# A post-norm decoder layer on one core: the queries' low part, the projection bias and the row scatters change their places

## What is computed

```python
x = _layernorm(x + _L0_attn_ref(x, ...))                 # a decaying linear attention, then a feed-forward
x = _layernorm(x + _L0_xattn_ref(x, ctx, ctx, mask, ...)) # 16 heads of 8 columns, softmax over the context
x = _layernorm(x + _L0_ffn_ref(x, Wr, W1, b1, W2, b2))    # 8 experts, the best 2 of each row
```

## Time and profile before

| | us |
|---|---|
| median of 3 runs | 801.77 |
| lowest, highest | 800.95, 807.67 |
| the profiled execution | 798.83 |
| its span | 797.0 |
| one loop pass (289.81 to 354.77) | 64.96 |
| TensorE busy, VectorE, ScalarE, GpSimd | 670.7, 512.8, 400.8, 320.8 |

### The profile page before, as it was taken

How to read it: one execution, slowest core, us unless ns; L and a number is a source line. 1 busy time by engine, 2 the same in 40 slices (tenths; PEclk the granted TensorE clock), 3 DMA queues, 4 the chain that set the end, 5 groups by cost and what they waited for, 6 DMA issues and landing times.

```text
span 797.0 us, 19859 instructions
## 1 busy us (share of the span) xinstructions
PE 670.7 (84%) x6190; PEld 502.2 (63%) x6190; DVE 512.8 (64%) x1733; ACT 400.8 (50%) x855; POOL 320.8 (40%) x463
## 2 busy tenths in 40 slices
PE   9789979888997987988888899798576999999920
PEld 9565636745854763764674585476353799999920
DVE  4687477767667768667676766766546355555535
ACT  0312555464474374465547347446240477777726
POOL 6104560363264165057136326405404255544535
PEclk8579997999998999899899899899575999999965
DMA  8500000000000000000000000000022222222144
GB/s 295 195 15 1 22 21 3 2 24 17 0 20 20 0 20 20 0 1 33 7 0 20 20 0 20 20 0 7 22 107 68 70 69 73 71 66 74 57 157 181
DMA packets 26058, 36.23 MB, mean 45 GB/s; under 512 B 7302, under 2 KB 18311, under 8 KB 25736
## 3 DMA queue, kind: packets, MB, share of 16 engines
q1 hardware_dynamic: 20582, 22.72, 9.2%
q0 software_dynamic: 4576, 9.53, 3.4%
q10 hardware_dynamic: 850, 3.38, 1.3%
HBM read 23.99 MB, written 12.63 MB: 46 GB/s over the span
## 4 chain that ended last, share of the span: by engine, by line
PE 53%; DVE 20%; issue 12%; POOL 5%; ACT 4%; DMA 2%; SPq 1%; another core or an unknown queue 1%; DVEq 1%; ACTq 0%; POOLq 0%
PE bank L1543 8%; PE bank L1858 8%; PE bank L1868 8%; PE bank L1708 4%; POOL rstd L737 3%; PE bank L1579 3%; PE bank L1677 3%; PE bank L1695 3%; DVE stats L1044 2%; ACT mix L555 2%; PE bank L1627 2%; PE bank L1716 2%; DVE negmax L1169 2%; PE bank L1635 2%; PE bank L1730 1%
## 5 line engine op out<-in xcount | busy, mean ns | idle before, releaser
L734 POOL TENSOR_SCALAR vare<-mv 128x1 f32<-128x1 f32 (+1 forms) x108 | 23.9, 221 | 267.2 <-DVE mv L1049 266.9
L856 POOL DMA_INDIRECT expert_out<-xa,v_sb x71 | 68.3, 962 | 77.2 <-issue 47.2
L675 ACT ACTIVATE hT<-bank,qT 128x128 f32<-128x128 f32 x284 | 81.0, 368 | 36.3 <-issue 19.8
L1169 DVE TENSOR_REDUCE negmax<-bank 128x4 f32<-128x512 f32 x128 | 80.2, 684 | 21.8 <-PE bank L1677 12.6
L555 ACT ACTIVATE mix<-bank 128x512 f32<-128x512 f32 x128 | 66.1, 603 | 36.9 <-PE bank L1695 36.6
L779 POOL DMA_INDIRECT expert_in<-xb_rows,slot_u x72 | 71.9, 999 | 31.1 <-issue 18.5
L1868 PE MATMUL bank<-w_t,hT 128*128 x568 | 75.5, 276 | 1.1 <-DVE xa L1389 0.5
L1858 PE MATMUL bank<-xnT,qT 128*128 128x128 f32 x568 | 75.1, 275 | 0.4 <-issue 0.4
L1868 PEld LDWEIGHTS bank<-w_t,hT 128*128 128x128 f32 x568 | 69.1, 192 | 2.0 <-issue 1.8
L737 POOL TENSOR_TENSOR rstd<-vare,minus_half 128x1 f32<-128x1 f32 (+1 forms) x108 | 66.5, 615 | 9.6 <-POOL vare L734 1.2
L1858 PEld LDWEIGHTS bank<-xnT,qT 128*128 128x128 f32 x568 | 69.0, 192 | 0.6 <-issue 0.6
(11 more groups left out here) (300 smaller groups left out, 1490.9 us busy)
## 6 DMA issues: line engine op xcount, KB each, us to landing
v_sb<-expert_in SPq DMA_DIRECT2D x71, 66.0 KB
w_t<-in_w_t ACTq DMA_DIRECT2D x1, 2064.0 KB, 7.5
x_all<-in_x SPq DMA_DIRECT2D x4, 512.0 KB, 7.7
xT_all<-in_xT SPq DMA_DIRECT2D x4, 512.0 KB, 8.3
ctxT<-in_ctxT SPq DMA_DIRECT2D x8, 256.0 KB, 2.9
w_t<-in_w_t SPq DMA_DIRECT2D x1, 2048.0 KB, 7.5
x_all<-expert_out SPq DMA_DIRECT2D x4, 512.0 KB, 10.0
mix<-expert_out SPq DMA_DIRECT2D x3, 512.0 KB, 7.4
```

The lines of the kernel that those rows point to most:

```text
L675: ins = nc.scalar.activation(hx[j % 2][:, c, :], bank[2 + j % 2][:, c * P:(c + 1) * P], ACT.Gelu, bias=w1c[j % 2][:, FF + c:FF + c + 1])
L856: nc.gpsimd.indirect_dma_start(ys[:, :], bass.IndirectOffsetOnAxis(ap=tag[j % ROWS][:, HOME - P:HOME - P + 1].bitcast(U32), axis=0), ysb[j ...
L1169: nc.vector.tensor_reduce(negmax[t % 2][:, i, 28:28 + XC], b[:, :].rearrange("p (c n) -> p c n", c=XC), AX.X, ALU.max, negate=True).then_i ...
```

## The change

On VectorE, `first_sums` can call a function when its four second sums are out and ahead of the statistics of tile 3 and the moments of tiles 2 and 3; in the seven loop passes `queries_low(g)` is called there, in the last group it stays where it was. On GpSimd, the eight scatters are issued one at a time with other work or a wait between them; three of the gaps hold a wait for a job of TensorE (`mx2i0`, `mT2`, `mT3`) and an increment of a semaphore that nobody reads; `xab` moves from behind the LNA scales to behind the fifth scatter and `ff_residual`.

```diff
-            def row_out(t):
-                for k in range(TOPK):
+            def row_out(t, ways=range(TOPK)):
+                for k in ways:
                     nc.gpsimd.indirect_dma_start(
                         xs[:, :], bass.IndirectOffsetOnAxis(ap=slot_u[:, t, k:k + 1], axis=0),
                         xb_rows[k][:, t, :], None).then_inc(scattered, 16)
...
             def group(g, last=False):
                 if not last:
                     first_sum_in(g + 2)
-                row_out(0)
+                row_out(0, [0])
                 if not last:
                     heb_residual(g + 1)
+                row_out(0, [1])
+                if not last:
                     gammas(g + 1)
                 ln_scale(LNA, g, 0)
                 ln_scale(LNA, g, 1)
                 ln_scale(LNA, g, 2)
                 ln_scale(LNA, g, 3)
+                row_out(1, [0])
+                if not last:
+                    ln_scale(LN2, g + 2, 0, T)
+                row_out(1, [1])
+                if not last:
+                    filled(pool, g, f"ks{XC - 1}")
+                    masks(g + 1)
+                row_out(2, [0])
+                if not last:
+                    ff_residual(g + 1)
                 pool.wait_ge(xn_ready[LNA], ln_nth(g, T - 1) + 1)
                 nc.gpsimd.tensor_tensor(
                     xab[:, :, :], xa[:, :, :],
                     bo_bc[:, :].unsqueeze(1).broadcast_to([P, T, P]), ALU.add).then_inc(xab_ready, 1)
                 if not last:
-                    ln_scale(LN2, g + 2, 0, T)
-                row_out(1)
-                row_out(2)
-                if not last:
-                    filled(pool, g, f"ks{XC - 1}")
-                    masks(g + 1)
-                row_out(3)
-                if not last:
-                    ff_residual(g + 1)
+                    filled(pool, g, "mx2i0")
+                pool.sem_inc(pool_held, 1)
+                row_out(2, [1])
+                if not last:
+                    filled(pool, g, "mT2")
+                pool.sem_inc(pool_held, 1)
+                row_out(3, [0])
+                if not last:
+                    filled(pool, g, "mT3")
+                pool.sem_inc(pool_held, 1)
+                row_out(3, [1])
+                if not last:
                     ln_scale(LN3, g + 1, 0)
...
-            def first_sums(k):
+            def first_sums(k, between=None):
...
                 for t in range(T + 2):
+                    if t == T and between:
+                        between()
                     if t < T:
...
                 def next_sums():
                     dve.wait_ge(x1b_ready, g + 2)
-                    first_sums(g + 2)
+                    first_sums(g + 2, lambda: queries_low(g))
...
                 if not last:
                     next_sums()
-                queries_low(g)
+                else:
+                    queries_low(g)
                 placed_queries(g, 1)
                 placed_queries(g, 3)
```

## The result

| | before | after |
|---|---|---|
| median | 803.13 (4 runs) | 768.02 (4 runs, 764.54 to 772.6) |
| the profiled execution, its span | 798.83, 797.0 | 772.6, 770.7 |
| loop passes (VectorE's loop branch to its next) | 64.5 to 65.6 | 60.2 to 60.4 |

All ratios here are the recorded ones, from executions in the fast state, and can differ a little from the quotient of the medians. The seven passes are 4.7 us shorter each, 33 us in all. The two profiled executions differ by 26 us only, because the last group and the expert phase took 5.6 us longer in that of the kernel after.

What follows compares the result with a forecast made beforehand. TensorE, busy 670.7 of 797.0 us, bounds the kernel, so gains come from its idle time. Seven passes at 1.34 us give 9.4: 789.4 from the profiled execution, 792.4 from the median, forecast 791, range 775 to 801.

Steps and rivals of the forecast that it cites:

- Part 1: VectorE's first sums (L1060): with `xab` gone from beside them, a hold of 1.03 us a pass ends.
- Part 2: VectorE: `low` ahead of three statistics and moments instructions can start 0.54 us earlier a pass; those three cost nothing.
- Together: `low` must wait for ScalarE's `high`, so it starts 1.34 us earlier; seven passes give 9.4 us, the last group 0.
- Part 3: GpSimd: scatters issued one at a time, later `xab` and three waits for TensorE change nothing: 0.
- the direct parts: Freeing the first sums from `xab` and moving `low` ahead of the moments: 9.4 us over seven passes.
- Rival (a): VectorE's stall before the second maxima, some 13.1 us, goes too once scatters are spread: 778 us; chance 0.12.
- (b): TensorE's low clock behind that stall shortens or goes: 9 us more gives 782, 18 more 773; chance 0.12.
- The low clock stays: The forecast kept the half-speed clock behind the second-maxima stall, costing about 2.6 us a pass; forecast's chance 0.55.
- Rival (d): The low clock lasts twice as long in each pass, over the attention work: 9 us slower, 809; chance 0.07.

Runs made afterwards that it cites:

- e2: Only `xab` moved, behind the packed scatters and `ff_residual`, against the kernel before on chip 3: 759.57 us, ratio 0.9893.
- e1: Only `queries_low` moved ahead of the last moments, GpSimd in its old order, against the kernel before on chip 3: 762.47 us, ratio 0.9928.
- e6: The whole change, unchanged, against the kernel before on chip 5: 758.74 us, ratio 0.9871.
- e11: Only the scatters issued one at a time with the three waits, `xab` and `low` unmoved, against the kernel before on chip 1: 777.09 us, ratio 0.9657.
- e12: The whole change without its three waits and increments, last three scatters in a row, against the kernel before on chip 1: 767.58 us, ratio 0.9545.
- e5: The kernel before, unchanged, run as a kernel of its own on chip 5: 769.38 us, ratio 0.9998.
- e8: Only the six packed scatters moved, behind the third turned maxima with one added wait, against the kernel before on chip 9: 846.27 us, ratio 1.0584.
- e10: The kernel before, unchanged, profiled on chip 9: 797.18 us in one execution.
- e7: `low` ahead of the moments and `xab` moved, scatters still packed, against the kernel before on chip 9: 794.98 us, ratio 0.9957.
- e15: The whole change without its three waits and increments, against the kernel before on chip 14: 768.47 us, ratio 0.9624.
- e13: The change with its scatters as four pairs instead of eight single ones, against the kernel before on chip 1: 801.49 us, ratio 0.9968.
- e14: The whole change once more, against the kernel before on chip 14: 765.91 us, ratio 0.9593.

## Why the prediction was wrong, point by point

- **Part 1, L1060 freed by `xab`: right.** The four take 1.13 us beside a scatter where 1.1 had been worked out; e2 alone brought 8.2 us where 7.2 were priced. The prediction also read the rule of the Trainium skill (SBUF — State Buffer, the practical consequences) strictly, so that a scatter's issue would block the sum as `xab` did. That reading did not hold: 1.13 us beside the scatter at 347.61.
- **Part 2, `low` ahead of the moments: right.** `low` starts 0.03 us behind `high` (0.1 forecast). e1 alone brought 5.5 us where 3.8 were priced. TensorE starts 0.51 us behind `low`, not 0.37.
- **Together, 9.4 us: right as far as it goes.** 9.9 us by e6's ratio, and a pass of 59.51 against 60.94 (1.43 for 1.34), on a chip without the stall.
- **Part 3, the scatters priced at 0: the step that failed.** Its working counted instructions, issue gaps and dependants of the scatters, and there it was right (3 waits hidden, `xab` early enough). It didn't count what packed scatters do to others: they delay TensorE's signals to VectorE and ScalarE, and VectorE's second maxima wait. Spacing alone is worth 25.0 us in e11; the direct parts' 9.4 to 9.9 on top make the 34.5 of e12 on the same chip (802.09 - 767.58).
- **Rival (a) is what happened, with (b) behind it.** (a) stood at 778 and (b) at up to 18 us more; each got 0.12, and their joint case no number. Two arguments against (a) were weak. The earlier trace rows show durations of VectorE's instructions beside scatters, but the hold is on a hand-off, which no duration shows; and those scatters start (765.1 - 631.7) / 70 = 1.9 us apart in the mean and take 0.96, which leaves some 0.95 us between two, against 0.30 in a packed row. "The same instruction in each pass" was taken as a mark of instruction fetch, yet GpSimd's order is as fixed as VectorE's. As the prediction read the Trainium skill's rule (Runtime: NRT & Kernel Launch, Instruction fetch mechanics), the stall would stay at that instruction; e5 runs the same loop without it, and e8 has the hold at other instructions and engines, so the rule does not explain it here.
- **The low clock stays: wrong.** It was expected to stay since one of two idle stretches stayed. Both went, or all but 0.3 us a pass. Its price of 2.6 us a pass was right: e10's pass has 57.38 - 54.74 = 2.64 us more of TensorE's busy time than e5's. For one pass, against e5, 64.96 - 60.94 = 4.0 us: 2.9 of busy time (57.65 - 54.74) and so only 1.1 of more idle, though the hold at the second maxima alone is 1.4; so some of what the slower matmuls took probably fell into waits for other engines, which no run separates.
- **Rival (d), slower, did not come**, but its mechanism shows in e7: with the direct parts alone the low clock grew (TensorE busy 58.79 against 57.38 in one pass, 680.4 against 672.3 in all) where 6 of some 10 us are missing.

A second, smaller hold of the same kind had been in the profile unread: the pair of scatters at the start of a pass. The first reader of the feed-forward's bank, before and then after:
```profile
359.55 0.29 DVE L1158 TENSOR_TENSOR x<-bank,xf 128x128 f32<-128x128 f32 x1 [2.91 <-PE bank L1730]
```
```profile
341.43 0.29 DVE L1175 TENSOR_TENSOR x<-bank,xf 128x128 f32<-128x128 f32 x1 [2.10 <-PE bank L1748]
```
and in e5, on chip 5, with the pair in place:
```profile
343.80 0.29 DVE L1158 TENSOR_TENSOR x<-bank,xf 128x128 f32<-128x128 f32 x1 [2.10 <-PE bank L1730]
```
That is 4.78, 3.98 and 3.98 us from the start of the pass: the pair costs 0.8 us where signals are late, and nothing on chip 5.

The change doesn't take all of the holds away. In the first comparison's changed kernel some of TensorE's signals are still up to 0.73 us late behind single scatters; its pass takes 60.24 us, against 59.51 in e6, and the medians are 766 to 768 us on three chips against 759 on chip 5. How much of these 7 to 9 us is the late signals' is not measured.

**What stays open.** Why chips 1, 9, 14 and that of the first comparison show late signals and chips 3 and 5 do not; which part of the chip delays them, and whether the recording of the profile has a share in it; and whether the stall causes the low clock or only comes with it. A stall at the second maxima and the low clock came and went together in the kernel before (e5, e10), e7, e11 and nearly all passes of the changed kernel. But e12 and e15 had a smaller hold at the third maxima (0.97 and 0.85 us) and no low clock, one pass of e13 had holds of that size and more and none, and one pass of e14 had 3.4 us of low clock (61.6 us instead of 60.2) without a stall at its maxima.

## What to carry to other kernels

Put other GpSimd work between two row scatters, and keep rows of them away from the places where VectorE or ScalarE wait for TensorE: on some chips they delayed TensorE's signals by 0.8 to 3.3 us at the hand-offs read here, and a fixed place in a loop makes it a stall in every pass. An idle stretch that the profile puts down to "remote", or to TensorE though its work was long done, is to be held against GpSimd's DMA issues in the same window. And a kernel that is slower on one chip than on another can have a cause that a change removes: compare the two traces pass by pass before pricing a part at nothing, and compare before and after on one chip only.

## What the runs showed of the hardware that was not expected

- The unchanged kernel takes 768 to 769 us on two chips and 797 to 803 on the others, 4% apart, steadily over 11 to 18 runs each (4 in the first comparison). The changed kernel takes 759 to 768 on the four on which it ran.
- Software-issued row scatters 0.30 us apart held TensorE's hand-offs: 1.4 us within a run of six, 1.6 in a pair, 2.7 and 3.3 in six without a break, on the chips that take about 800 us. With other work between them the same eight leave no idle at the second maxima; single late signals of up to 0.73 us remain. ScalarE's hand-off to TensorE in the same stretch took 0.14 us, and the signals of VectorE, ScalarE and GpSimd were never over 0.013 us late.
- Where TensorE's signals were late, they came in bursts: in e8 four of them within 0.10 us, 1.1 us behind the last scatter, up to 6.89 us late. The same traces lack 80 to 382 of 768 records of landed scatters.
- On a chip that shows holds, removing 1.3 us of idle time elsewhere in the pass (e7) came with a longer low clock, not a shorter one: 0.92 granted in the pass against e10's 0.95.
